# Four engines' order of work set anew within a pass of the local-attention layers (one core, Trainium2)

## The reference

```
x_s = shift_tokens(x)                         # channels 64.. come from the token before
q, k, v = split(x_s @ Wqkv)                   # 16 heads of 64
q, k = rotary(l2norm(q)), rotary(l2norm(k))
out = softmax(8 q k^T over the own window of 32 tokens and the one before) v
x = x + out @ Wo
h = layernorm(shift_tokens(x)) @ W1 + b1 ;  a, gate = split(h)
x = x + (a * gelu(gate)) @ W2 + b2            # 341 hidden channels
```

## Time and profile before

| | us |
|---|---|
| median of 3 runs | 4588.0 (4586.9 to 4590.96) |
| the profiled execution, its own time | 4585.71 |
| its span in the trace | 4583.9 |
| 46 passes, from the `fold` product of pass 1 to that of pass 47 | 3180.59 |
| one pass in the steady state | 69.30 |

### The profile page before, as it was taken

The page is one execution under the profiler, slowest core; times in us unless marked ns, Lnnn a source line. Parts: engine busy times, 40 slices in busy tenths (PEclk is TensorE's granted clock), DMA queues, the critical chain, the costliest instruction groups (busy, mean ns, idle before and its releaser), DMA issues. The chain is left out here.

```text
span 4583.9 us, 117843 instructions
## 1 busy us (share of the span) xinstructions
PE 4024.2 (88%) x43247; PEld 2378.6 (52%) x43247; DVE 3549.3 (77%) x8496; ACT 2985.7 (65%) x5496; POOL 2213.8 (48%) x1392
## 2 busy tenths in 40 slices
PE   8969999999999999999999999999999954747645
PEld 5644555555555555555555555555555532535533
DVE  6878888888888888888888888888888846356441
ACT  3427777777777777777777777777777745635302
POOL 0006665666666666666566666656656500140006
PEclk9989999999999999999999999999999965868557
DMA  1012322322223322232222322233222200000202
GB/s 42 1 55 64 67 59 62 83 66 64 61 61 84 69 61 62 60 85 68 60 61 63 83 67 63 59 77 72 63 62 66 55 17 12 1 1 6 83 7 38
DMA packets 188120, 251.24 MB, mean 55 GB/s; under 512 B 88676, under 2 KB 129382, under 8 KB 187366
## 3 DMA queue, kind: packets, MB, share of 16 engines
q1 hardware_dynamic: 182054, 240.47, 22.5%
q0 software_dynamic: 5632, 4.33, 0.7%
HBM read 41.65 MB, written 14.30 MB: 12 GB/s over the span
## 5 line engine op out<-in xcount | busy, mean ns | idle before, releaser
L1246 POOL TENSOR_TENSOR f_rot_a<-f_rot_a,f_norm 128x1024 f32<-128x1024 f32 x384 | 730.8, 1903 | 947.2 <-DVE f_norm L1085 914.7
L1238 POOL TENSOR_TENSOR f_rot_a<-f_rot_a,f_rot_b 128x1024 f32<-128x1024 f32 x384 | 909.5, 2368 | 229.7 <-issue 197.2
L843 PE MATMUL f_bank<-f_w_vo,f_xs_t 128*32 128x512 f32 x6144 | 813.7, 601 | 42.6 <-ACT f_vo L1315 42.6
L1315 ACT ACTIVATE f_vo<-f_bank 128x512 f32<-128x512 f32 x768 | 457.0, 595 | 357.7 <-PE f_bank L843 347.4
L1306 ACT ACTIVATE f_squares<-f_bank 128x512 f32<-128x512 f32 x768 | 456.4, 594 | 271.6 <-PE f_bank L829 191.5
L1064 DVE TENSOR_TENSOR f_rot_a<-f_bank,f_rot 128x512 f32<-128x512 f32 x768 | 523.7, 682 | 80.4 <-DVE f_stat L1113 42.2
L1067 DVE TENSOR_TENSOR f_rot_b<-f_bank,f_rot 128x512 f32<-128x512 f32 x768 | 516.0, 672 | 0.0
L875 PEld LDWEIGHTS f_bank<-f_k_t,f_q_t 128*32 128x32 f32 x12288 | 329.1, 110 | 284.7 <-ACT f_k_t L1327 151.5
L1071 DVE TENSOR_REDUCE f_sums<-f_squares 128x16 f32<-128x1024 f32 x384 | 464.0, 1208 | 1.6
L1327 ACT ACTIVATE f_k_t<-f_bank 64x512 f32<-64x512 f32 x768 | 449.3, 585 | 4.8 <-PE f_bank L865 0.3
L1252 POOL TENSOR_TENSOR f_prob<-f_score,f_stat 128x512 f32<-128x512 f32 x384 | 400.1, 1042 | 96.4 <-DVE f_stat L1117 96.4
(11 more groups left out here) (446 smaller groups left out, 7227.1 us busy)
## 6 DMA issues: line engine op xcount, KB each, us to landing
f_vo_off<-f_vo SPq DMA_DIRECT2D x1152, 128.0 KB, 2.3
f_vo_off<-f_vo SPq DMA_DIRECT2D x384, 64.0 KB, 2.0
f_w_qk<-in_Wqk SPq DMA_DIRECT2D x12, 512.0 KB, 5.2
f_vo_dram<-f_vo_pair SPq DMA_DIRECT2D x48, 128.0 KB, 1.8
f_x_shifted<-s_all SPq DMA_DIRECT2D x48, 128.0 KB
f_x_shifted<-s_all SPq DMA_DIRECT2D x48, 127.0 KB
f_w_vo<-f_vo_dram SPq DMA_DIRECT2D x10, 512.0 KB, 4.0
e_w<-in_e_W SPq DMA_DIRECT2D x2, 2048.0 KB, 11.6
```

The costliest lines, as they stand in the source:

```text
L843: done = nc.tensor.matmul(bank[V][32 * w:32 * w + 32, :], x[:, at:at + 32], w_vo[:, 4 * g:4 * g + 4, w // 2, :], start=True, stop=True)
L1238: nc.gpsimd.tensor_tensor(rot_a[:, slot, :, :], rot_a[:, slot, :, :], rot_b[:, g, :, :], ALU.add).then_inc(rot_summed, 1)
L1246: nc.gpsimd.tensor_tensor(heads, heads, over(norm[:, 16 * g:16 * g + 16], [128, 16, HEAD_DIM]), ALU.mult).then_inc(qk_normed, 1)
L1315: nc.scalar.activation(vo[:, g, 2 * (t % 2) + j, :], flat(V), ACT.Copy).then_inc((va_copied, vb_copied)[j], 1)
```

## The change

The lists in `body(p)` of PE, DVE, POOL and ACT are written out flat and in another order. Every step is still there once for each pass, tile and group, with the same waits and the same operands. SP's list changes in one place: `shift_x` now stands between the two calls of `shift_values(p, 1, g)` instead of behind them. `normalise` is cut into two halves of two tiles each; DVE's list calls them one right behind the other. The lines of the new kernel stand further down in its file (PE's by 1, DVE's by 93 to 94, POOL's by 196, ACT's by 213).

```diff
@@ SP, one_pass @@
                     if r > 0 or q > 0 or not first:
                         shift_values(p, r - 1, 0)
+                    if r == 2 and (q > 0 or not first):
+                        shift_x(p - 1, (q - 1) % PASSES)
+                    if r > 0 or q > 0 or not first:
                         shift_values(p, r - 1, 1)
...
-                    if r == 2 and (q > 0 or not first):
-                        shift_x(p - 1, (q - 1) % PASSES)
@@ PE, body @@
-                for r in range(PASS_TILES):
...
-                    if on(r):
-                        project_k(p, r, 0)
...
+                if live(p, -1):
+                    turn_q(p, -1, 0)
+                if live(p, 0):
+                    project_k(p, 0, 0)
+                    project_q(p, 0, 0)
...
@@ DVE @@
-            def normalise(p):
-                if live(p + 2, 0):
-                    dve.wait_ge(norms_made, count(p + 2, 1))
-                else:
-                    chain.wait()
-                if has(p, 1):
-                    dve.wait_ge(f_turned, p)
-                for t in range(PASS_TILES):
+            def normalise(p, half):
+                if half == 0:
+                    if live(p + 2, 0):
+                        dve.wait_ge(norms_made, count(p + 2, 1))
+                    else:
+                        chain.wait()
+                    if has(p, 1):
+                        dve.wait_ge(f_turned, p)
+                for t in (2 * half, 2 * half + 1):
...
-                last.then_inc(f_normed, 1)
+                if half == 1:
+                    last.then_inc(f_normed, 1)
...
+                if has(p, 2):
+                    normalise(p - 2, 0)
+                    normalise(p - 2, 1)
+                if has(p, 3):
+                    store(p - 3)
```

More of the change, by code:

```diff
@@ L1161, in body @@
             def body(p):
[L1162 to L1215, removed]
@@ new lines, in body @@
+                if live(p, -2):
+                    total(p, -2, 1)
+                if live(p, -3):
+                    residual(p, -3)
+                if live(p, 0):
+                    rotate(p, 0, 0, 1, 0)
+                    rotate(p, 0, 0, 0, 0)
+                    rotate(p, 0, 0, 1, 1)
+                if live(p, -2):
+                    invert(1)
+                if live(p, 0):
+                    rotate(p, 0, 0, 0, 1)
+                    length(p, 0, 0)
+                if has(p, 3):
+                    hide(p - 3, 2)
@@ new lines, in body @@
+                if live(p, 1):
+                    highest(p, 1, 1)
+                if live(p, 3):
+                    rotate(p, 3, 0, 0, 0)
+                    rotate(p, 3, 0, 0, 1)
+                if live(p, 1):
+                    total(p, 1, 1)
+                if live(p, 3):
+                    length(p, 3, 0)
+                if live(p, 0):
+                    residual(p, 0)
+                if live(p, 1):
+                    invert(1)
+                if has(p, 1):
+                    statistics(p - 1)
@@ L1216, in body @@
+                if live(p, 2):
+                    highest(p, 2, 1)
+                    total(p, 2, 0)
+                if has(p, 2):
+                    hide(p - 2, 1)
+                if live(p, 2):
+                    invert(0)
                 chain.reset()
@@ L1254, in body @@
             def body(p):
[L1255 to L1273, removed]
+                if has(p, 0):
+                    take_x(1, p)
@@ new lines, in body @@
+                if live(p, 0):
+                    square(p, 0, 1, 1)
+                    square(p, 0, 1, 0)
+                if live(p, -1):
+                    exponential(p, -1, 0)
+                if has(p, 0):
+                    copy_fold(p)
+                if live(p, -1):
+                    copy_q(p, -1, 1)
+                    copy_values(p, -1, 1, 1)
+                if live(p, -2):
+                    copy_prob(p, -2, 1)
+                if live(p, -1):
+                    seed(p, -1, 1)
+                    copy_k(p, -1, 1)
@@ new lines, in body @@
+                if has(p, 0):
+                    shift_in(1, p)
+                if live(p, 1):
+                    square(p, 1, 0, 1)
+                if live(p, 0):
+                    copy_values(p, 0, 0, 0)
+                    copy_q(p, 0, 0)
+                if live(p, 1):
+                    square(p, 1, 0, 0)
+                if live(p, -1):
+                    exponential(p, -1, 1)
+                if live(p, 0):
+                    copy_values(p, 0, 0, 1)
+                    copy_k(p, 0, 0)
+                    seed(p, 0, 0)
+                    copy_values(p, 0, 1, 0)
@@ new lines, in body @@
+                if live(p, 0):
+                    seed(p, 0, 1)
+                    exponential(p, 0, 0)
+                if has(p, 2):
+                    take_gate(p - 2, 0)
+                if live(p, 1):
+                    copy_values(p, 1, 0, 0)
+                if live(p, -1):
+                    copy_prob(p, -1, 1)
+                if live(p, 1):
+                    copy_q(p, 1, 0)
+                if live(p, 2):
+                    square(p, 2, 0, 0)
+                if live(p, 0):
+                    exponential(p, 0, 1)
@@ new lines, in body @@
+                if live(p, 2):
+                    square(p, 2, 1, 1)
+                if live(p, 1):
+                    copy_values(p, 1, 0, 1)
+                    seed(p, 1, 0)
+                    copy_k(p, 1, 0)
+                if live(p, 2):
+                    square(p, 2, 1, 0)
+                if live(p, 0):
+                    copy_prob(p, 0, 0)
+                if live(p, 1):
+                    copy_values(p, 1, 1, 0)
+                if has(p, 2):
+                    take_gate(p - 2, 1)
@@ new lines, in body @@
+                if live(p, 1):
+                    copy_q(p, 1, 1)
+                if live(p, 0):
+                    copy_prob(p, 0, 1)
+                if live(p, 1):
+                    exponential(p, 1, 0)
+                    copy_values(p, 1, 1, 1)
+                    copy_k(p, 1, 1)
+                if has(p, 2):
+                    take_gate(p - 2, 2)
+                if live(p, 3):
+                    square(p, 3, 0, 1)
+                if live(p, 1):
+                    seed(p, 1, 1)
@@ new lines, in body @@
+                if live(p, 3):
+                    square(p, 3, 0, 0)
+                if has(p, 2):
+                    gelu(p - 2)
+                if live(p, 2):
+                    copy_values(p, 2, 0, 0)
+                if live(p, 1):
+                    exponential(p, 1, 1)
+                if live(p, 2):
+                    copy_q(p, 2, 0)
+                if live(p, 3):
+                    square(p, 3, 1, 1)
+                if has(p, -1):
+                    shift_in(0, p + 1)
@@ L1419, in _ @@
+                if live(p, 3):
+                    copy_values(p, 3, 0, 0)
+                if live(p, 2):
+                    exponential(p, 2, 0)
             stream(act, body)
```

446 lines of the change are left out of this document (335 added, 111 removed).

## The result

| | before | changed | |
|---|---|---|---|
| median of 4 runs each, us | 4589.48 | 4461.73 (4456.33 to 4462.0) | ratio 0.9719 [0.9704, 0.9733] |
| profiled execution, its own time | 4585.71 | 4456.33 | |
| its span | 4583.9 | 4454.5 | -129.4 |
| up to the first of the 46 passes | 403.07 | 414.35 | +11.3 |
| the 46 passes, `fold` to `fold` | 3180.59 | 3045.19 | -135.4 |

The account below looks back on a forecast made before the run. The prediction took TensorE as the bound, busy 67.25 of 69.30 us a steady pass. Saving 1.95 us in each of 46 passes gives 90 us less, 4496, plus 2.3 for the median: 4498 us, range 4472 to 4550.

Parts of the forecast that it names:

- TensorE's own time: TensorE's busy time in a steady pass, taken as unchanged by the new order at 67.25 us, 0.3 either way.
- 2.05 of waits go: TensorE's four recurring waits in a steady pass (V21a, S20, U1, `turn_normed`), 2.05 us together, claimed to go nearly whole.
- the GELU lump: ScalarE's table load and three GELU operations, 2.87 us a pass, claimed to cause TensorE's waits at V21a and S20.
- The count of changes between 32 and 128 columns: TensorE's changes from narrow to wide products in a pass, which cost a little: 16 before and 16 after.
- The 0.15 left on S20: Part of TensorE's 0.60 us wait for `seed` at S20 expected to stay each pass, as ScalarE has nothing in hand.
- the 0.05 for slips: Allowance of 0.05 us a pass for TensorE starting late at V21a and U0.
- The layout of ScalarE: ScalarE's computed times from G2 on: spare of 1.4 us at V20b, 0.4 at U0, 0.2 at V21a, 0 to 0.1 at S20.
- The ends: The first two and last three passes of the list, not dense, taken as unchanged with 8 us either way.
- Rival 1: ScalarE is 0.2 us late at five tight places (U0, V21a, S20, S11, S10): 46 us back, 4544 us; chance 0.15.
- Rival 2: `normalise` on VectorE held up three times by GpSimd, 6.1 instead of 3.4 us, delaying Q11: 4576 us; chance 0.06.
- Rival 3: TensorE's waits only move to other late steps and come to 2 us a pass again: 4588 us; chance 0.05.
- Rival 4: VectorE, own time 63.5 us a pass, becomes the bound through waits such as `total`: slower, 4634 us; chance 0.10.

## Why the prediction was right and wrong

- **The step that failed** is the one on TensorE's own time: "I take TensorE's own time as unchanged at 67.25; it could be 0.3 shorter or longer". With it went the bound that an order of work "can't take away any of the 67.25". 67.25 was its busy time, and 1.2 us of that were waits. TensorE alone takes 66.06 with the old list and 65.83 with the new. So the term "2.05 of waits go" should have been 3.24 - 0.03, with 0.24 from the order of the blocks on top. Shown: both own times, 0.07 to 0.16 us beyond each listed wait, 0.06 to 0.10 behind two of them, and 0.09 to 0.15 at four places with none listed. The mechanism (the waits of the earlier trace rows go, since the GELU lump is covered) was right; the size of its term was not. The count of changes between 32 and 128 columns held (the lists differ by 0.24, inside the 0.3).
- The 0.15 left on S20 and the 0.05 for slips did not come. The layout of ScalarE was right, to 0.2 us at V20b and to 0.1 at S20; I had not believed it fully.
- **The ends** were costed as unchanged with 8 us either way: they came out at +11.3 and -5.3, together +6.0. Of the 11.3, 8.5 lie between the first two `fold` products (64.20 us for 55.66). The -5.3 is less than two traces of one kernel differ by there (1006.1 and 994.4, above). The changes of layer were not in the sum at all. They cost 19 us over steady passes, and the reason could have been seen: whatever moves K and the rotations forward in a pass asks for the next layer's loads sooner.
- Sum by measured terms: the passes give 3180.59 - 3027.69 = 152.9 when the long ones are taken out (the kernel with earlier loads), the long ones take 17.5 back and the ends 6.0: 129.4. The forecast had 90 for all of it. The forecast gave the passes 63 too little, of which a steady pass explains 1.19 (hidden waits) + 0.24 (order of the blocks) + 0.10 (kept back for S20 and slips) - 0.03 = 1.50, which is 69 in 46 passes; the passes that are not steady gave less (the first two of the 46 gave 1.4 us together, where two steady ones give 6.9). The range's lower bound doesn't follow from its terms either: 4588 - 46 x 2.4 - 8 is 4470, not 4472; the time lies below both.
- **`normalise`** was put at 2.5 to 4 us with 3.4 taken; it took 2.7 at its new place (median of 45). The rows, VectorE's and GpSimd's beside it:

```profile
1548.45 1.04 POOL L1433 TENSOR_TENSOR f_prob<-f_score,f_stat 128x512 f32<-128x512 f32 x1
1549.44 1.92 POOL L1427 TENSOR_TENSOR f_rot_a<-f_rot_a,f_norm 128x1024 f32<-128x1024 f32 x1
1549.27 2.70 DVE L1237 TENSOR_SCALAR f_f_n<-f_x_shifted,f_f_mv,f_norm 128x128 f32<-128x128 f32 x4
```

The second of its four operations waits out the `scale` of 1.92, the other three take a third of a microsecond each; before, two were held up (1.93 and 1.08, by `scale` and `weigh`). Of 180 single operations the median is 336 ns where it was 710, the longest 1940. The Trainium skill (SBUF — State Buffer, Who interferes with whom) has VectorE in a two-port mode and GpSimd hold their shared pair of ports exclusively, each for a whole instruction. The trace agrees (1.93 against 0.34 us), and at the place now chosen one operation is held up, not three.
- **VectorE**: no wait for `x_shifted`, 1.54 us at `total` where 1.4 was laid out. Its own time, by the prediction's method, is (3045.19 - 149.3) / 46 = 62.95 us a pass, the span less all its listed waits (149.3), below the 65.86 of TensorE.
- **Rival 1** (slips of ScalarE): not so here, but its mechanism is real; one operation more cost 0.52 a pass, with all of it at three of the five places named. **Rival 2** (`normalise` held up three times): wrong, see above. **Rival 3** (the waits only move): wrong for the steady pass, right in small for the changes of layer. **Rival 4** (VectorE the bound): wrong, but close; 2.1 us of wait for `x_shifted` a pass cost 1.0, so VectorE has 1.1 in hand, and by estimate from these two numbers the kernel would be slower than before from about 1.1 + 3.4 = 4.5 us more of waits on VectorE.

## What to carry to other kernels

Where TensorE looks 97% busy, ask what its list takes by itself: issue the same products in the same order on operands that never change, and compare start to start, block by block; the difference to that, and what a new order takes less by itself (0.24 us here), is what a better order can win. A static order spread over five engines is one piece: judge it as a whole, by laying out the tight places from a trace's durations, since one engine's list alone can lose several times the gain. And look at the passes that are not like the others (a new layer's loads), whose cover an earlier step takes away.

## What the runs showed of the hardware

Waits of TensorE are partly counted as busy. Four waits set by hand cost 0.62 us a pass beyond their listed length, 0.15 each on average, and a stall of 0.52 us a pass, spread over three places, was listed at no matmul. In TensorE's list alone a values block took 0.86 to 0.88 us ahead of a block on 32 columns and 0.97 to 1.00 ahead of one on 128. A load of ScalarE's table took 1.28 us, and the next operation started 0.01 behind its end (1511.76 + 1.28, then 1513.05). The start of a weight load, and the distance from block start to block start, show what the matmul rows hide.
